# Eight-headed attention: outputs moved ahead of scores on TensorE, two PSUM banks for outputs and four for scores

## The reference

```python
def _L1_xattn_ref(x, context, Wq, Wk, Wv, Wo, bo):
    H = 8; D = 64; SCALE = D ** (-0.5)
    q = (x @ Wq).reshape(B, Nq, H, D)
    k = (context @ Wk).reshape(B, Nkv, H, D)
    v = (context @ Wv).reshape(B, Nkv, H, D)
    sim = jnp.einsum('bihd,bjhd->bhij', q, k) * SCALE
    attn = jax.nn.softmax(sim, axis=-1)
    out = jnp.einsum('bhij,bjhd->bihd', attn, v).reshape(B, Nq, H * D)
    return out @ Wo + bo
...
x = x + _L1_xattn_ref(_layernorm(x), ctx_768, ...)
x = x + _L1_ffn_ref(_layernorm(x), ...)
```

## Time and profile before

| what | us |
|---|---|
| median of three runs | 989.41 |
| the profiled execution, its own time | 991.27 |
| its span | 989.5 |
| TensorE busy in the span | 834.5 (84%) |
| VectorE busy in the span | 770.0 (78%) |
| ScalarE busy in the span | 650.7 (66%) |
| first score matmul of this stage | 691.87 |
| first matmul of the next stage | 820.55 |

### The profile page before, as it was taken

The page is one execution under the profiler, slowest core; times in us unless marked ns, Lnnn a source line. Parts: engine busy times, 40 slices in busy tenths (PEclk is TensorE's granted clock), DMA queues, the critical chain, the costliest instruction groups (busy, mean ns, idle before and its releaser), DMA issues. The chain is left out here.

```text
span 989.5 us, 23134 instructions
## 1 busy us (share of the span) xinstructions
PE 834.5 (84%) x9198; PEld 540.3 (55%) x9198; DVE 770.0 (78%) x1404; ACT 650.7 (66%) x1155; POOL 378.2 (38%) x384
## 2 busy tenths in 40 slices
PE   1387879798579889999968999998889958999997
PEld 0122323232246645655635776766778745778786
DVE  7999989934568988888858999996899936667443
ACT  4578789987558645544328888886889836656431
POOL 1042444332136413000027888886465502224220
PEclk9997889898759989999979999999999989999999
DMA  5402414050041021000031000000456520000000
GB/s 153 85 2 34 53 28 61 6 82 1 3 168 44 1 98 42 1 2 1 1 136 40 3 4 2 3 3 2 103 101 106 96 47 1 1 12 12 12 23 32
DMA packets 57962, 39.70 MB, mean 40 GB/s; under 512 B 42288, under 2 KB 54270, under 8 KB 56704
## 3 DMA queue, kind: packets, MB, share of 16 engines
q1 hardware_dynamic: 55104, 35.61, 16.8%
q10 hardware_dynamic: 2752, 2.62, 0.9%
HBM read 18.56 MB, written 2.10 MB: 21 GB/s over the span
## 5 line engine op out<-in xcount | busy, mean ns | idle before, releaser
L589 ACT ACTIVATE t_pT<-t_sc 128x1536 f32<-128x1536 f32 x96 | 136.8, 1454 | 29.3 <-PE t_sc L696 29.0
L269 POOL TENSOR_SCALAR_AFFINE_SELECT t_pT<-t_pT 128x512 f32<-128x512 f32 x64 | 73.8, 1174 | 170.2 <-ACT t_pT L589 170.2
L696 PE MATMUL t_sc<-t_qk 32*128 32x512 f16 (+3 forms) x1152 | 90.3, 369 | 45.5 <-DMA t_qk<-t_sin_parts 25.2
L696 PEld LDWEIGHTS t_sc<-t_qk 32*128 32x128 f16 x1152 | 37.1, 100 | 106.4 <-issue 51.3
L717 PE MATMUL t_ot<-t_pT,t_v 128*17 128x512 f32 (+3 forms) x768 | 83.1, 545 | 10.6 <-DVE t_ou L433 4.6
L2837 POOL TENSOR_SCALAR_AFFINE_SELECT r_att<-r_att 128x1024 f16<-128x1024 f16 x64 | 68.7, 1098 | 25.4 <-DVE r_att L2886 25.4
L2052 PE MATMUL c_pso<-ck_VO,c_pT 128*128 128x256 f16 x480 | 59.8, 287 | 14.5 <-DVE x L1881 14.5
L2052 PEld LDWEIGHTS c_pso<-ck_VO,c_pT 128*128 128x128 f16 x480 | 48.8, 103 | 23.5 <-issue 15.8
L2339 ACT ACTIVATE m_sg<-m_psg 128x512 f32<-128x512 f32 x32 | 19.1, 596 | 56.5 <-PE m_psg L2382 56.4
L1956 ACT ACTIVATE c_pt<-c_pss,c_mx 128x154 f32<-128x154 f32 x128 | 48.6, 410 | 4.5 <-DVE c_mx L1852 4.5
L2403 PE MATMUL m_acc<-gw_down,m_hp 128*128 128x256 f16 x384 | 47.2, 273 | 2.4 <-DVE m_hp L2295 2.0
(11 more groups left out here) (628 smaller groups left out, 2412.6 us busy)
## 6 DMA issues: line engine op xcount, KB each, us to landing
t_qk<-t_cos_parts SPq DMA_DIRECT2D x24, 128.0 KB, 5.2
t_qk<-t_sin_parts SPq DMA_DIRECT2D x24, 128.0 KB, 6.8
x<-in_x ACTq DMA_DIRECT2D x4, 512.0 KB, 6.0
out_x<-x SPq DMA_DIRECT2D x8, 256.0 KB, 2.1
r_rcos<-in_ret_cos SPq DMA_DIRECT2D x1, 1280.0 KB, 8.2
r_rsin<-in_ret_sin SPq DMA_DIRECT2D x1, 1280.0 KB, 10.4
t_qk<-t_cos_parts SPq DMA_DIRECT2D x16, 64.0 KB, 2.7
gw_raw<-in_gateT SPq DMA_DIRECT2D x1, 1024.0 KB, 7.2
```

What stands on the lines that cost most here:

```text
L269: last = g.affine_select(out=blk, in_=blk, compare_op=ALU.is_ge, fill=0.0, base=0, pattern=[[0, 4], [1, P]], channel_multiplier=-1)
L589: a.activation(pT[:, at:at + 3, :].rearrange("p a s -> p (a s)"), sc[s % 2][:], ACT.Exp, scale=CURVE * CURVE / math.sqrt(2 * DH)).then_inc ...
L696: last = t.matmul(sc[s % 2][:, 512 * k + at:512 * k + at + w], qk[r, g % 3, 1, of_k, P * i:P * i + P], qk[r, g % 3, 0, of_q, q0:q0 + w], s ...
```

## The change

- PSUM: `pso` has two banks, used by turns (tile t in bank t % 2), and the ring of score banks has four instead of five. `output(t)` waits for the sum of tile t - 2 (`x_done` at t - 1) where it waited for that of tile t - 1. A score's banks wait for one more group of exponentials.
- TensorE: from step 3 on, `output(s - 2)` is the first of the step and `score(s + 1)` the last, behind the row turns. In step 1, tile 0's weights are turned before `score(2)`. Tile 15's are turned at the end of step 15 (before: in step 16, ahead of `output(14)`).
- VectorE: `add` stands behind the maxima and ahead of `x_low`, `beside` and `part_low`, up to step 15; then at the end as before. Four row statistics stand ahead of the loop, the others and the spreads of both `opening` and `rows` some steps sooner; `rows.low(2)` is in step 16 and `rows.low(3)` at the end of step 17.
- Next rows: turned in steps 14 (tiles 0 and 1) and 15 (2 and 3), where it was 14, 15, 15 and 16. `rows.high(2)` and `rows.high(3)` are in steps 15 and 16 behind the copies.
- GpSimd: in steps 2 to 5 the second expanded piece of weights waits for `parted`, so that it doesn't run beside `part_low`; the powers come some steps sooner.

No instruction is added or taken away but waits.

```diff
@@ -1747,7 +1747,7 @@
-    RING, LAST = 5, NT - 1
+    RING, LAST = 4, NT - 1
@@ -1762,7 +1762,7 @@
-        psx, psq, pss, pso = ps("psx", [P, 512]), ps("psq", [P, 512]), ps("pss", [P, RING, 512]), ps("pso", [P, 512])
+        psx, psq, pss, pso = ps("psx", [P, 512]), ps("psq", [P, 512]), ps("pss", [P, RING, 512]), ps("pso", [P, 2, 512])
@@ -1770,7 +1770,7 @@
-        TURN_AT = {NT - 2: (0,), NT - 1: (1, 2), NT: (3,)}
+        TURN_AT = {NT - 2: (0, 1), NT - 1: (2, 3)}
@@ -1819,17 +1819,17 @@
-                signs.on_gpsimd(g, own, s)
+                signs.on_gpsimd(g, s, parted)
...
-                if s in (10, 14):
-                    rows.power(g, (s - 10) // 4)
+                if s in (10, 13):
+                    rows.power(g, (s - 10) // 3)
@@ -1903,29 +1902,35 @@
+            for t in range(10, 14):
+                opening.statistic(v, own, t)
             for s in STEPS:
                 maxima(s, 0)
                 weigh(s - 1)
                 maxima(s, 1)
                 maxima(s, 2)
+                if s == 2:
+                    add(0)
+                if 3 < s <= LAST:
+                    add(s - 3)
                 x_low(s + 2)
                 beside(s)
                 part_low(s - 1)
-                if s == 2:
-                    add(0)
-                if s > 3:
+                if s > LAST:
                     add(s - 3)
                 for j in range(3):
                     p_low(s - 1, j)
+                if s == LAST + 2:
+                    rows.low(v, own, 3)
@@ -2046,28 +2049,36 @@
-                    wait(t_, x_done, t)
+                    wait(t_, x_done, t - 1)
                     todo = [(pT[:, q, pa, k, :], keys.VO[:, pw, b, k, :]) for k in range(SLOTS) for pa, pw in three]
                     for n, (l, r) in enumerate(todo):
-                        last = mm(pso[:, 0:D], l, r, start=(n == 0), stop=(n == len(todo) - 1))
+                        last = mm(pso[:, q, 0:D], l, r, start=(n == 0), stop=(n == len(todo) - 1))
                     last.then_inc(out_ready, 1)
 
             for s in STEPS:
-                score(s + 1)
-                for j in range(3):
-                    turn_p(s - 1, j)
+                if s > 2:
+                    output(s - 2)
+                elif s != 1:
+                    score(s + 1)
+                if s == 1:
+                    for j in range(3):
+                        turn_p(0, j)
+                    score(2)
                 project(s + 2)
                 turn_x(s + 3)
-                if s == 1:
-                    output(0)
-                if s > 2:
-                    output(s - 2)
                 for t in TURN_AT.get(s, ()):
...
                     rows.turn(t_, t, ROW_BANKS[t % 2], signs.id16, t - 1)
+                if s == 1:
+                    output(0)
+                if s > 2:
+                    score(s + 1)
+                if s == LAST:
+                    for j in range(3):
+                        turn_p(LAST, j)
@@ -3298,11 +3309,13 @@
             for c in (2 * s - 4, 2 * s - 3):
+                if c % 2:
+                    g.wait_ge(parted, s - 1)
```

More of the change, by code:

```diff
@@ L1783, in turned @@
         def turned(t, j):
-            return (pso, psq, pso)[j][:] if t == 0 else pss[:, (3, 4, 0)[j]]
+            return (pso[:, 0], psq[:], pso[:, 1])[j] if t == 0 else pss[:, j]
         def landings(t):
@@ L1821, in _ @@
                 weigh_rest(s - 1)
-                if s == 5:
+                if s == 3:
                     opening.power(g, 2)
-                signs.on_gpsimd(g, own, s)
+                signs.on_gpsimd(g, s, parted)
                 if MIX_FROM <= s < MIX_FROM + 2 * signs.PIECES:
@@ L1880, in add @@
                     v.wait_ge(out_ready, t + 1)
-                    v.scalar_tensor_tensor(x[:, t, :], pso[:, 0:D], 1.0 / XSCALE, x[:, t, :], ALU.mult, ALU.add).then_inc(x_done, 1)
+                    v.scalar_tensor_tensor(x[:, t, :], pso[:, t % 2, 0:D], 1.0 / XSCALE, x[:, t, :], ALU.mult, ALU.add).then_inc(x_done, 1)
             def beside(s):
@@ L1885, in beside @@
                     signs.scales(v)
-                if s in (1, 2):
-                    opening.statistic(v, own, 2 * s + 8)
-                    opening.statistic(v, own, 2 * s + 9)
+                if s == 1:
+                    opening.statistic(v, own, 14)
+                    opening.statistic(v, own, 15)
+                if s == 2:
+                    opening.spread(v, own, 2)
                 if s in (3, 4):
-                    opening.statistic(v, own, s + 11)
                     signs.on_vector(v, s - 3)
-                if s == 5:
-                    opening.spread(v, own, 2)
-                if s == 6:
+                if s == 4:
                     opening.offsets(v, 2)
@@ L1905, in beside @@
                     rows.offsets(v, 0)
-                if s in (12, 13):
-                    rows.low(v, own, s - 12)
+                if s == 12:
+                    rows.spread(v, own, 1)
+                if s in (13, 14):
+                    rows.low(v, own, s - 13)
                 if s == 14:
-                    rows.spread(v, own, 1)
-                if s == 15:
                     rows.offsets(v, 1)
-                if s in (16, 17):
-                    rows.low(v, own, s - 14)
+                if s == 16:
+                    rows.low(v, own, 2)
+            for t in range(10, 14):
+                opening.statistic(v, own, t)
             for s in STEPS:
@@ L1990, in _ @@
                     rows.high(a, s - 11)
-                if s in (16, 17):
-                    rows.high(a, s - 14)
                 for t in TURN_AT.get(s, ()):
                     rows.copy(a, t, ROW_BANKS[t % 2])
+                if s in (15, 16):
+                    rows.high(a, s - 13)
         @block.tensor
@@ L3299, in on_vector, with on_gpsimd @@
             v.tensor_tensor(self.w[0][:, s], self.k[0][:, s], self.k[0][:, 2 + s], ALU.subtract).then_inc(self.differed, 1)
-    def on_gpsimd(self, g, own, s):
+    def on_gpsimd(self, g, s, parted):
         if 2 <= s < 2 + C1 // 2:
```

2 lines of the change are left out of this document (removed).

## The result

The changed kernel takes 1020.9 us (median of four runs, 1018.9 to 1022.8), the kernel before 989.9 beside it: a ratio of 1.031 (95% interval 1.028 to 1.034). The prediction was 1014.0 us, in a range of 1001 to 1022. The profiled execution took 1021.7 us, with a span of 1019.9.

The account below looks back on a forecast made before the run. TensorE was taken as full in the middle, idle only at the end; head cost 6.9, middle cost 28.2, end gain 10.5: 24.6 us on 991.27, or 1015.9, with the median 1.86 lower: 1014.0 us, range 1001 to 1022.

Parts of the forecast that it names:

- the loop: Score, maxima, low part, transfer, output, score: 16.38 us plus side work per two steps, against TensorE's own 12.48.
- The middle: D(4) to D(14), steps 4 to 14: five double steps and slow outputs, 94.1 us against 65.85 before, cost 28.2.
- D(s): Start of VectorE's step s, its first maxima; the mark by which the forecast cut the stage.
- the list: VectorE's side work in even steps of the middle: 1.4, 0, 0.66, 0.66 and 1.39 us, less 0.2.
- The clock: TensorE's clock falls behind each long gap before an odd output, adding 1.66 us to that output.
- half-price reading: Skill's figure of about 1.67 us throttled per pass, half lost: seven gaps cost about 5.8 us, total 1008.2.
- The head: Up to D(4): the first sum waits for output 0 and holds the low part; cost 6.9 us.
- The end: D(14) to the next stage: outputs 13 to 15 no longer wait for a sum; 26.4 us against 36.9, gain 10.5.
- The ring of four: Four score banks instead of five: scores wait for the second exponentials, thin cover, costed at nothing.
- The transfers: Each tile's transfer in the loop: issue 0.03 and landing 4.9 us, the median of 14; by the skill's page 4.5.
- the rival of slower transfers: Transfers slower than the median: at 5.7 us each the seven in the chain add 5.6, total 1019.6; 15%.
- The clock did not hold: Answers the rival that the clock stays up behind the gaps: 11.6 us go, total 1002.4; 14%.

Follow-up runs that it names:

- both edits: Changed kernel with the sum and side work moved behind the low part on VectorE, and each tile's transfer in two halves: 1001.6 us.

## Why the prediction was right

**What bounds the kernel, and the loop: shown.** Idle time stands before the seven odd outputs and ends with a landing; even outputs have next to none, as forecast. The seven gaps sum to 30.9 us, 4.4 each, where the text said 3.9 or more. Changing one term moved the gaps by nearly that term (a landing 1.5 us shorter, gaps 1.3 shorter), and taking the loop away by the order alone gave back 21 us.

**The middle: +29.9 for +28.2.** The five double steps took 20.19, 18.72, 19.23, 18.21 and 19.44 us. Of their excess over 16.38, 10.2 is the slow outputs (their time over 3.44 us) and 3.7 the rest, for which I had 8.3 and 3.9. The term that was too small is the **clock**. That the rest came out so near is in part luck, because two misses met. VectorE's time from D(s) to the end of its low part was 6.2, 5.1, 5.7, 5.7 and 6.4 us in steps 4 to 12, which is 3.0 us of side work over 5 x 5.21 where the list has 4.1. Against that, one transfer was slow: tile 5's low part ended at 753.44, and its output began at 759.61, 6.2 us later, where the term is 4.9.

```profile
751.95 1.49 DVE L1870 TENSOR_TENSOR c_ph<-c_pn,c_ph 128x1280 f16<-128x1280 f32 x1
```


**The clock: mis-sized, 1.66 for 2.24 us.** The seven outputs behind gaps took 4.74 to 6.31 us, 5.68 on average. I took 5.10, the slowest that the rows showed, and called 1.66 the upper bound; outputs here went over it by up to 1.2 us. Within this kernel the length of the gap doesn't order them (3.81 us was followed by 5.93, 4.49 by 4.74). Holding the clock up was worth 12.2 us of the stage, and 7 x 1.66 is 11.6, which looks better than it is: the seven excesses sum to 15.7, the slow output 10 of that kernel takes 1.7 back, and the other 1.8 are open. The half-price reading of the Trainium skill ("TensorE: Matmul & The Clock Gate", HAM oscillation), an estimate of 0.83 us for each pass, is further off: that section's shape is the one seen here, its size is not.

**The head: +8.2 for +6.9.** The excess is the slow output 1, 6.04 us instead of 5.10, and output 0 ending 0.4 us later. The step in the text, that the first sum would now wait for output 0 and hold the low part, is there (2.19 us on VectorE at 711.08).

**The end: -9.9 for -10.5.** The order of events is as worked out. The last gap is 4.96 us and its output takes 6.28 instead of 5.10; the terms around it (VectorE's step, the turns) came out 0.6 us shorter in all and hide half of that.

**The ring of four: right for this order only.** By the trace it costs next to nothing in the changed kernel, and 10 us under the order of before. Had the forecast been asked of that combination, the same sentence would have been wrong.

**The transfers.** The changed kernel has 4.8 to 6.5 us with the median of 4.9, as before. Half the bytes land in 3.4 us; if the time is a fixed part and one by size, and the two halves don't hinder each other, half costs 1.5 us (328 KB, an estimate of some 220 GB/s) and the fixed part is 1.9. The Trainium skill, "DMA: Bandwidth & Descriptors", in its cost components, has about 2.0 us for the fixed part, fitted to transfers issued from GpSimd; the estimate for these, issued from SyncE, is near it. Its 261 GB/s for a transposing transfer, in the section on latency and other measured facts, is more than was seen here.

**The number and the rivals.** The time came out near the rival of slower transfers (1019.6), but not by its mechanism: one transfer of the seven in the chain was slow, by 1.2 us, where that rival adds 5.6. The clock did not hold. Of the 6.9 us between forecast and median 3.6 are the stage. 2.2 are earlier stages, which the change doesn't touch and which ended that much later in this execution; the other executions here began this stage anywhere from 688.5 to 693.5. The last 1.1 is how the profiled executions stand to their medians.

## What to carry to other kernels

When work is reordered so that an engine's step begins with something that comes back through a DMA, write down the loop before anything else: who makes its input, in which step, and what stands last in the step that waits. If the sum over the loop exceeds the engine's own work for the steps it spans, the difference is idle time; in the changed kernel it collected before one output of two, and TensorE's work behind it was slow. A resource that is free in one order (a PSUM bank) can be the bound in the next one, so its cost belongs to an order and not to an edit. And a wait that stands only at the end of a stage is best mended at the end: an arrangement of the end alone won 11 us here (989.9 to 978.8), and the change, which reordered every step, lost 31.

## What the runs showed that I had not expected

- The clock didn't follow the length of the last gap alone. Gaps of 2.42 us in one kernel and 2.31 in the earlier trace rows were followed by outputs of 5.12 and 5.10 us, and one of 2.22 in the kernel with the extra matmuls by 5.11; but gaps of 2.60 in the earlier trace rows, 2.72 with the low part sooner and 2.14 with both edits were followed by 3.44 and 3.45. Gaps of 1.1 us before every output left it at 1.00.
- The same loop ran in two ways in one execution, with the idle time in equal parts or before one output of two, and the first was over 2 us faster in a double step. What made it go from one to the other (side work on VectorE in one step is my guess) I did not try.
